# Routing of a group laid over two attention blocks, in an attention and mixture-of-experts kernel

## The chip, the cores and the metric

The kernel runs on one core of one Trainium2 chip. The metric is the device time of one execution in microseconds (us). The engines are PE (TensorE: matmuls), ACT (ScalarE), DVE (VectorE), POOL (GpSimd) and SP (SyncE, which issues most of the DMAs here).

## What is computed

```
qkv = x @ qkv_w + qkv_b                       # x: 2 x 2048 x 256, 16 heads of 16
q, k rotated; attn = softmax(q k^T / 4)       # 32 heads of 2048 x 2048
x1 = layernorm(x + (attn v) @ out_w + out_b)
n = layernorm(x1) * g1 + be1
x2 = x1 + n + (n @ mix_w + mix_b)
n2 = layernorm(x2) * g2 + be2
probs = softmax(n2 @ router_w)                # 8 experts, the best two are kept
out = sum over the two of p * (silu(n2 @ w1[e] + b1[e]) @ w2[e] + b2[e])
result = layernorm(x1 + x2 + out)             # "x1 +": residual around the whole second part
```

The 4096 tokens are sent to a table of rows sorted by expert; the experts then work on 71 tiles of 128 such rows.

## The kernel before, in words

**Phases.** `project` makes q, k and v, `maxima` is skipped for these inputs, and `attend_route_experts` does the rest: attention with the routing woven in, then the expert tiles, then the last norm. All of it is written out by hand: every engine has its own list of instructions, and semaphores join them.

**Attention.** The tokens are eight groups of 512. A block `i` is attention for group `i`: four units (quads of heads) of 32 steps, 128 steps `n` in all. At step `n` PE waits for exponential `n`, computes the scores of step `n + 3` (`score`, L1409, 8 matmuls into one of three PSUM buffers), and at every second step weighs one round of values (`weigh`, L1421, 4 matmuls that are recorded as 8, into the one output bank `at_po`). ACT does one exponential of 128x1024 a step (L1316). When a unit is weighed, DVE copies the output bank (`copy_out`, L1629) and later divides (`divide`: shuffle, reciprocal, product, L1637 to L1641). The first round of the next unit is weighed at its third step (g = 2) and needs that copy. SP then moves the unit into `heads_T` (`repack`, L995).

**Routing.** While block `i` runs, group `i - 1` is routed. On PE the routing is cut into pieces, each put after a step by a table: `OUT_AT` (eight pieces of the output product, two halves of four), `NORM_AT` (two transposes), `MIX_AT` (eight pieces), `SENT_AT` (two transposes of the second norm's rows), `ROUTER_AT` (two pieces of logits), `COUNT_AT` (counts). All share one PSUM bank, `small`; a job in it may start when DVE has read the one before (`small_read`). DVE's `route` adds each half to `total`, does three norms (`layer_norm`, L702 to L728), and chooses experts and places. POOL adds biases and residuals, copies values of the next unit (`copy_v`), and sends the rows by eight indirect DMAs (L1208). ACT does the router's exponential after step 104.

**After attention.** The last group's routing is set between expert tiles by `TAIL_AT`: a point `2i + 1` stands in tile `i` behind the first product of tile `i + 1` (`hide`, L1540), a point `2i + 2` behind tile `i`'s second product (`reduce`, L1553). A tile needs 1 MB of `w1`, in a ring of three, and 129 KB of rows. SP issues the weights of tile 2, then `b2`, then `repack` of the last unit, then the weights of tiles 3, 4 and 5 (L1078). 36 tiles are planned early, from the counts of groups 0 to 5 (`plan_early`).

Of the kernel before, what the change touches and what calls it, by code (L numbers as in the profile page):

```python
# [8 lines left out]
ALU = mybir.AluOpType  # L9
# [11 lines left out]
QC = S // 512  # L21
# [740 lines left out]
def attend_route_experts(nc, dram, keep):  # L762
# [14 lines left out]
    OUT_AT = {14: (0, 0), 16: (0, 1), 18: (0, 2), 20: (0, 3), 24: (1, 0), 28: (1, 1), 32: (1, 2), 33: (1, 3)}  # L777
    NORM_AT = {54: 0, 56: 1}
    MIX_AT = {60: (0, 0), 62: (0, 1), 64: (0, 2), 65: (0, 3), 68: (1, 0), 72: (1, 1), 76: (1, 2), 80: (1, 3)}
    SENT_AT = {92: 0, 94: 1}  # L780
    ROUTER_AT = {97: 0, 98: 4}
    COUNT_AT = 118
    LATE_V_FROM, LATE_V_EVERY = 8, 7
    with ExitStack() as stack:
# [128 lines left out]
        def piece(g):  # L913
# [19 lines left out]
        STEPS = 3 * LN_STEPS + 19  # L933
# [31 lines left out]
        def first_job(i):  # L965

            return LATE_JOBS + (i - 1) * JOBS
# [8 lines left out]
        with nc.Block() as block:  # L976

            @block.sync
            def _(sp):
# [5 lines left out]
                def repack(unit):  # L985
# [5 lines left out]
                    if i:  # L991
                        sp.wait_ge(small_done, first_job(i) + 2)
# [45 lines left out]
                for c in range(1, QC - 1):  # L1038
                    for q in range(UNITS):
                        load_q(0, c, q, c * UNITS + q)  # L1040
                        repack(c * UNITS + q - 2)
                    load_x(c)
                    keep_sum(c - 1)
                for q in range(UNITS):
# [3 lines left out]
                    repack((QC - 1) * UNITS + q - 2)  # L1048
                load_x(QC - 1)
                keep_sum(QC - 2)  # L1050
                load_second_k(1)
                sp.wait_ge(keep["stored_mid"][1], 16 * QC)
                for q in range(UNITS):
                    load_q(1, 0, q, QC * UNITS + q)
                    repack(QC * UNITS + q - 2)
                    if q < 2:
                        load_second_k(q + 2)
                load_x(QC)
                keep_sum(QC - 1)
# [23 lines left out]
                for c in range(1, QC - 1):  # L1083
                    for q in range(UNITS):
                        load_q(1, c, q, (c + QC) * UNITS + q)
                        repack((c + QC) * UNITS + q - 2)
                    load_x(c + QC)
                    keep_sum(c + QC - 1)

                for q in range(UNITS):  # L1090
                    load_q(1, QC - 1, q, LAST * UNITS + q)
                    repack(LAST * UNITS + q - 2)
                load_x(LAST)
# [5 lines left out]
                keep_sum(LAST - 1)  # L1099
# [13 lines left out]
                load_w1(2, 2)  # L1113
                sp.wait_ge(weighed, GROUPS * NR + LEAD)
# [56 lines left out]
            def _(pool):  # L1171
# [14 lines left out]
                def route(i, q):  # L1186

                    if q == 1:
                        pool.wait_ge(norm1_ready, i + 1)
# [776 lines left out]
```

## Time and profile before

| | us |
|---|---|
| three timed runs | 1661.41, 1660.91, 1659.82 (median 1660.91) |
| the profiled execution | 1657.93 |
| its span, first to last instruction | 1656.2 |
| attention, first exponential to the start of the last | 108.6 to 1089.6 |
| PE / ACT / DVE / POOL busy | 1601.3 / 1249.5 / 540.8 / 470.3 |

The profile records one execution. Its page gives busy time by engine, the chain of work that ended last, and the costliest groups of instructions; views of the trace give timelines, waits and sums over stretches. Matmul records overlap, since matmuls are pipelined, so how long a run of them holds PE is read from the starts of one run and the next, not from their lengths.

### The profile page before, as it was taken

The page shows a single profiled execution, that of the slowest core. Times are in us where ns is not written, and L with a number is a line of the kernel's source. Part 1 is how long each engine was busy: PE and PEld are TensorE (multiplying, and loading weights), DVE is VectorE, ACT ScalarE, POOL GpSimd, SP SyncE. Part 2 cuts the span into 40 slices and gives each one's busy share as a digit, 9 for nine tenths or more (in the row PEclk, how much of TensorE's full clock was granted, in tenths as well). Part 3 has the DMA queues.
Part 4 walks back from the last instruction along what each step waited for, and adds up shares of the span by engine and source line. Part 5 has one row for each costly group of instructions (what it writes and reads, how often), then busy time and mean ns, then how long its engine had stood idle before and what let it go on. Part 6 is the DMA issues. An engine that isn't in the chain of part 4 may idle for free.

```text
span 1656.2 us, 46008 instructions
## 1 busy us (share of the span) xinstructions
PE 1601.3 (97%) x18036; PEld 948.0 (57%) x18037; DVE 540.8 (33%) x1464; ACT 1249.5 (75%) x1879; POOL 470.3 (28%) x495
## 2 busy tenths in 40 slices
PE   7989999999999999999999999999999999999991
PEld 5544434434434434434433434468999999999990
DVE  5541215525525525515615535526110000000004
ACT  5669999999999999999999999953434444444442
POOL 4630011212212212212212212125455444444441
PEclk9999999999999999999999999999999999999996
DMA  5686110101102551300101101646577765666655
GB/s 175 204 174 88 47 41 11 54 28 28 53 28 67 92 92 39 105 29 28 53 28 31 50 28 34 242 162 179 161 198 203 201 188 166 187 181 173 186 136 209
DMA packets 108488, 181.20 MB, mean 109 GB/s; under 512 B 14121, under 2 KB 80361, under 8 KB 108137
## 3 DMA queue, kind: packets, MB, share of 16 engines
q1 hardware_dynamic: 94515, 160.47, 33.7%
q0 software_dynamic: 13296, 17.77, 5.5%
q8 instruction: 130, 2.13, 0.6%
q10 hardware_dynamic: 495, 0.41, 0.1%
q14 instruction: 52, 0.43, 0.1%
HBM read 134.07 MB, written 40.18 MB: 105 GB/s over the span
## 4 chain that ended last, share of the span: by engine, by line
PE 68%; issue 13%; DVE 5%; POOL 3%; ACT 2%; DMA 2%; POOLq 1%; DVEq 0%; ACTq 0%
PE at_s L1409 23%; PE at_po L1421 22%; PE at_s L1540 8%; PE at_s L1553 8%; PE at_small L1437 4%; ACT place L1316 2%; DMA rows_out<-place,at_v 1%; POOL place L1275 1%; PE at_small L1430 1%; POOL place L1270 1%; DVE cb_ln_stats L702 1%; DVE rt_ln_stats L702 1%; DVE rt_sent_rows L728 1%; PE at_po L1529 1%; DVE rt_sent_rows L1693 1%
## 5 line engine op out<-in xcount | busy, mean ns | idle before, releaser
L1316 ACT ACTIVATE place<-at_s 128x1024 f32<-128x1024 f32 x1024 | 956.4, 1112 | 25.9 <-PE at_s L1409 18.6
L1409 PE MATMUL at_s<-place 99*32 99x512 bf16 x8192 | 579.7, 380 | 6.5 <-PEq L614 3.8
L1421 PE MATMUL at_po<-place,at_v 128*32 128x512 f32 x4096 | 535.8, 593 | 0.0
L1409 PEld LDWEIGHTS at_s<-place 99*32 99x32 bf16 x8192 | 219.4, 96 | 442.1 <-issue 237.9
L1333 ACT ACTIVATE place<-at_s,b_turned 128x128 f32<-128x128 f32 x568 | 161.6, 368 | 141.5 <-PE at_s L1540 139.3
L1540 PEld LDWEIGHTS at_s<-ex_xT,place 128*128 128x128 f32 x2272 | 264.3, 192 | 5.8 <-issue 1.7
L1540 PE MATMUL at_s<-ex_xT,place 128*128 128x128 f32 x2272 | 265.7, 275 | 0.0
L1553 PE MATMUL at_s<-place 128*128 x1136 | 257.1, 379 | 1.0 <-issue 0.5
L1553 PEld LDWEIGHTS at_s<-place 128*128 128x128 f32 x1136 | 210.4, 190 | 27.4 <-issue 1.7
L1421 PEld LDWEIGHTS at_po<-place,at_v 128*32 128x32 f32 x4096 | 132.3, 110 | 96.1 <-issue 1.2
L1349 ACT ACTIVATE place<-at_s,at_v 128x256 f32<-128x256 f32 x71 | 33.6, 474 | 161.5 <-PE at_s L1553 158.4
L702 DVE BATCH_NORM_STATS2 cb_ln_stats<-place 128x6 f32<-128x256 f32 x32 | 10.7, 411 | 417.0 <-DMA place<-rows_out 417.0
L1175 POOL COPY at_v<-place 128x1024 f32<-128x1024 f32 x32 | 33.2, 1038 | 306.1 <-PE at_po L1421 258.8
L1280 POOL DMA_INDIRECT rows_out<-place,at_v x71 | 115.8, 1631 | 14.5 <-issue 13.2
L1208 POOL DMA_INDIRECT rows_in<-rt_sent_rows,rt_pos x64 | 62.3, 974 | 162.6 <-PE at_po L1421 157.1
L1639 DVE RECIPROCAL at_den<-at_den 128x512 f32<-128x512 f32 x32 | 107.3, 3353 | 1.1
L1270 POOL TENSOR_TENSOR place<-place,at_v 128x256 f32<-128x256 f32 x71 | 80.4, 1132 | 40.1 <-PE at_po L1529 36.6
L1653 DVE TENSOR_TENSOR late<-at_small,rt_total 128x512 f32<-128x512 f32 x32 | 22.1, 692 | 203.3 <-PE at_small L1437 203.3
L1275 POOL TENSOR_TENSOR place<-place 128x256 f32<-128x256 f32 x71 | 52.5, 739 | 81.6 <-ACT place L1349 78.7
L1629 DVE COPY at_o<-at_po 128x512 f32<-128x512 f32 x32 | 22.1, 692 | 159.9 <-PE at_po L1421 159.9
L1196 POOL TENSOR_TENSOR rt_total<-late 128x1024 f32<-128x1024 f32 x7 | 16.8, 2400 | 185.2 <-DVEq L1687 185.2
L1279 POOL TENSOR_TENSOR ex_spare_y<-rt_zero_rows 128x1 f32<-128x1 f32 x71 | 15.4, 217 | 173.3 <-DMA rows_out<-place,at_v 171.9
(222 smaller groups left out, 1022.8 us busy)
## 6 DMA issues: line engine op xcount, KB each, us to landing
place<-in_w SPq DMA_DIRECT2D x79, 1024.0 KB, 9.4
place<-k_parts SPq DMA_DIRECT2D x48, 256.0 KB, 4.6
place<-q_parts SPq DMA_DIRECT2D x186, 64.0 KB
at_v<-rows_in SPq DMA_DIRECT2D x71, 129.0 KB
place<-in_x SPq DMA_DIRECT2D x8, 512.0 KB, 4.7
at_heads_T<-at_o SPq DMA_DIRECT2D x128, 32.0 KB, 2.0
rt_x_in<-in_x SPq DMA_DIRECT2D x8, 512.0 KB, 4.1
rows_out<-rt_total SPq DMA_DIRECT2D x8, 512.0 KB, 3.9
```

The source lines that it names most:

```text
L1208: nc.gpsimd.indirect_dma_start(out=dram["rows_in"], in_=sent_rows[:, n, a, :], in_offset=None, out_offset=bass.IndirectOffsetOnAxis(ap=pos ...
L1270: nc.gpsimd.tensor_tensor(biased[:, :], b2[:, bass.ds(e, 1), :].rearrange("p o n -> p (o n)"), rows_now[:, r, D + 1:D + 2].broadcast_to([P ...
L1275: nc.gpsimd.tensor_tensor(y[:, u, :], y[:, u, :], biased[:, :], ALU.add).then_inc(y_ready, 1)
L1280: nc.gpsimd.indirect_dma_start(out=dram["rows_out"], in_=y[:, u, :], in_offset=None, out_offset=bass.IndirectOffsetOnAxis(ap=rows_now[:, r ...
L1316: nc.scalar.activation(probs[:, slot(i, n), :], scores(i, n)[:, :], ACT.Exp).then_inc(exp_done, 1)
L1333: last = nc.scalar.activation(hT[:, u, fc, :], p_h[u][:, fc, :], ACT.Silu, bias=keep["b1"][:, bass.ds(e, 1), fc])
L1409: last = nc.tensor.matmul(scores(i, n)[j:j + 32, s * 512:(s + 1) * 512], k_rows[0:ROWS_M, quad(q).start + h, kt * P + j:kt * P + j + 32], ...
L1421: last = nc.tensor.matmul(p_o[32 * h:32 * h + 32, :], v_one[q % 2][:, h, kt, :], probs[:, slot(i, q * NG + g), s * 512:(s + 1) * 512], sta ...
L1437: last = nc.tensor.matmul(out[j:j + 32, :], weights[:, j:j + 32], moving, start=start, stop=stop, skip_group_check=lone)
L1540: last = nc.tensor.matmul(p_h[u][:, fc, :], w1_now[slot][:, kc, fc * P:(fc + 1) * P], xT[:, u, kc, :], start=(kc == 0), stop=(kc == KC - 1))
L1553: last = nc.tensor.matmul(p_y[u][:, :], hT[:, u, fc, :], w2[:, bass.ds(e, 1), fc, :].rearrange("p o n -> p (o n)"), start=(fc == 0), stop= ...
L1639: v.reciprocal(den[:, :], den[:, :]).then_inc(den_ready, 1)
```

## The change

In block `i` two groups are now routed at once, each by a part. The front of group `i - 1` (output product, two norms, mixing, sums) stands at steps 24 to 56 and 80 to 116. The back of group `i - 2` (transposes of the second norm's rows, logits, counts) stands at steps 10 to 20 and at 40. Nearly all pieces are four steps apart. Block 1 has a front alone. After attention the back of group 6, then front and back of group 7 are set between expert tiles. The same operations are done, and each once for each group.

```diff
-    OUT_AT = {14: (0, 0), 16: (0, 1), 18: (0, 2), 20: (0, 3), 24: (1, 0), 28: (1, 1), 32: (1, 2), 33: (1, 3)}
-    NORM_AT = {54: 0, 56: 1}
-    MIX_AT = {60: (0, 0), 62: (0, 1), 64: (0, 2), 65: (0, 3), 68: (1, 0), 72: (1, 1), 76: (1, 2), 80: (1, 3)}
-    SENT_AT = {92: 0, 94: 1}
-    ROUTER_AT = {97: 0, 98: 4}
-    COUNT_AT = 118
+    SENT_AT = {10: 0, 14: 1}
+    ROUTER_AT = {18: 0, 20: 4}
+    ROUTER_EXP_AT = 27
+    COUNT_AT = 40
+    OUT_AT = {24: (0, 0), 28: (0, 1), 32: (0, 2), 36: (0, 3), 44: (1, 0), 48: (1, 1), 52: (1, 2), 56: (1, 3)}
+    NORM_AT = {80: 0, 84: 1}
+    MIX_AT = {88: (0, 0), 92: (0, 1), 96: (0, 2), 100: (0, 3), 104: (1, 0), 108: (1, 1), 112: (1, 2), 116: (1, 3)}
...
-        TAIL_AT = {3: (14, 16, 18, 20), 4: (24, 28, 32, 33), 9: (54,), 10: (56,), 11: (60, 62, 64, 65),
-                   12: (68, 72, 76, 80), 17: (92,), 18: (94,), 19: (97, 98), 26: (118,)}
-        SEND_ROUNDS = {0: (3, 5, 8, 10, 13, 15), 1: (18, 21)}
-        ROUTER_AFTER, SEND_AFTER = 10, 15
+        TAIL_AT = {3: ((LAST - 1, 10),), 4: ((LAST - 1, 14),), 5: ((LAST - 1, 18), (LAST - 1, 20)),
+                   7: tuple((LAST, at) for at in (24, 28, 32, 36)), 11: ((LAST - 1, COUNT_AT),),
...
+        FIRST_SENDS, LAST_SENDS = (25, 27, 29, 31), (34, 36, 42, 44)
+        ROUTER_AFTER = {3: LAST - 1, 15: LAST}
+        SEND_AFTER = {LAST - 1: 5, LAST: 18}
...
                 sp.wait_ge(scored, 2 * NG + LAST * NB + NB)
                 load_w1(2, 2)
+                keep_sum(LAST - 1)
                 sp.wait_ge(weighed, GROUPS * NR + LEAD)
                 sp.dma_start(b2[:, :, :], dram["b2"].partition_broadcast(P)).then_inc(loaded_b2, 16)
                 repack(GROUPS * UNITS - 1)
...
+                def route(i):
+
+                    beside = i < GROUPS
+                    front, back = i - 1, i - 2
+                    if back >= 0:
+                        choose(back)
+                    if beside:
+                        copy_out(i, 0)
...
+                    add_total(x1, 0)
+                    if back >= 0:
+                        give_places(back)
+                    if beside:
+                        divide(i, 0)
+                    if i == LAST:
+                        plan_early(nc, dve, making, carry, keep, scratch, planned)
+                    add_total(x1, 1)
...
+                    layer_norm(v, steps, x1, x1, w)
+                    if beside:
+                        copy_out(i, 1)
+                    layer_norm(v, steps, norm1, x1, w)
...
+                    if i == LAST:
+                        dve.wait_ge(x_turned, 2)
+                        v.tensor_copy(xT[:, :, :, :], p_x_first[:, :, :, :]).then_inc(xT_ready, 2)
+                        copy_out(i, 3)
+                    dve.wait_ge(sent, front + 1)
+                    layer_norm(v, steps, sent_rows[:, 0, :, 0:D], x2, w)
+                    if i < LAST:
+                        copy_out(i, 3)
+                    steps.then(v.tensor_tensor(norm1[:, :, :], sent_rows[:, 0, :, 0:D], spread("g2"), ALU.mult))
+                    v.tensor_tensor(sent_rows[:, 0, :, 0:D], norm1[:, :, :], spread("be2"), ALU.add
+                                    ).then_inc(norm2_ready, 1)
...
+                    if beside:
+                        divide(i, 3)
```

`repack` in a block now waits for six jobs of `small`, not two, since the output product ends at step 56 instead of 33. POOL's loop has the same operations in another order (`add_bias` and `double` at the start of a block, the sends between rounds 25 and 44).

How the instructions stand on three engines, names as in the program (`at_s` scores, `at_po` output bank, `at_small` the routing bank, `place` the large buffer of keys, probabilities and weights):

PE, the first two pieces of the output product in a block, before:

```order
L1437 MATMUL at_small<-rt_out_w,at_heads_T 32x256 x3
L1409 MATMUL at_s<-place 32x512 [waits at_exp_done]
L1409 MATMUL at_s<-place 32x512 x7
L1421 MATMUL at_po<-place,at_v 32x512 x4
L1409 MATMUL at_s<-place 32x512 [waits at_exp_done]
L1409 MATMUL at_s<-place 32x512 x7
L1437 MATMUL at_small<-rt_out_w,at_heads_T 32x256 x4
```

and now:

```order
L1467 MATMUL at_small<-rt_out_w,at_heads_T 32x256 x3
L1439 MATMUL at_s<-place 32x512 [waits at_exp_done]
L1439 MATMUL at_s<-place 32x512 x7
L1451 MATMUL at_po<-place,at_v 32x512 x4
L1439 MATMUL at_s<-place 32x512 [waits at_exp_done]
L1439 MATMUL at_s<-place 32x512 x7
L1439 MATMUL at_s<-place 32x512 [waits at_exp_done]
L1439 MATMUL at_s<-place 32x512 x7
L1451 MATMUL at_po<-place,at_v 32x512 x4
L1439 MATMUL at_s<-place 32x512 [waits at_exp_done]
L1439 MATMUL at_s<-place 32x512 x7
L1467 MATMUL at_small<-rt_out_w,at_heads_T 32x256 x4
```

The pieces were two steps apart and are four apart.

DVE, at the end of the last attention block, from the copy of the first expert rows on, before:

```order
L1794 COPY ex_xT<-at_small 128x512 [waits ex_x_turned]
L1629 COPY at_o<-at_po 128x512 [waits at_repacked1,at_weighed]
L1637 STREAM_SHUFFLE at_den<-at_o 128x512 [waits at_o_normed,at_o_copied]
L1639 RECIPROCAL at_den<-at_den 128x512 [waits at_den_ready]
L1641 TENSOR_TENSOR at_o<-at_o,at_den 128x512 [waits at_den_ready]
```

and now, first where the copy stands (18 short instructions of the norm lie between this place and the next):

```order
L1786 COPY ex_xT<-at_small 128x512 [waits at_small_read,ex_x_turned]
L1659 COPY at_o<-at_po 128x512 [waits at_repacked1,at_weighed]
L702 BN_STATS rt_ln_stats<-late 128x6 [waits rt_sent]
L702 BN_STATS rt_ln_stats<-late 128x6 x3
L715 TENSOR_TENSOR rt_ln_mean<-rt_ln_stats 128x4 [waits rt_step]
```

The second place, where the division stands:

```order
L728 TENSOR_SCALAR rt_sent_rows<-late,rt_ln_rstd,rt_ln_shift 128x256 x3
L1792 TENSOR_TENSOR late<-rt_sent_rows,rt_g 128x1024 [waits rt_step]
L1793 TENSOR_TENSOR rt_sent_rows<-late,rt_be 128x4x256 [waits rt_step]
L1667 STREAM_SHUFFLE at_den<-at_o 128x512 [waits at_o_normed,at_o_copied]
L1669 RECIPROCAL at_den<-at_den 128x512 [waits at_den_ready]
L1671 TENSOR_TENSOR at_o<-at_o,at_den 128x512 [waits at_den_ready]
```

The whole second norm of group 6 now stands between the copy and the division of the last unit.

SP, from the weights of tile 2 to those of tile 3, now:

```order
L1090 DMA place<-in_w 128x2x1024
L1016 DMA rows_out<-rt_total 128x4x256 [waits rt_kept]
L1130 DMA place<-in_b 128x2048 [waits at_weighed]
L1004 DMA at_heads_T<-at_o 16x512 [waits at_small_done,at_o_normed]
L1004 DMA at_heads_T<-at_o 16x512 x3
L1086 TENSOR_LOAD tile_expert
L1090 ISA [waits ex_hidden]
```

Before, the same stood there without the store of the kept sum (L1016): the weights of tile 3 are issued behind `repack`, which waits for the division (`at_o_normed`).

## Rows read from the trace of the kernel before

**Rows 1.** Windows, exponentials alone (L1316): block 1 and block 4: length, ACT busy (count)

```profile
227.96:350.89 122.93, 119.41 (x129) 1.00 0.10 28
...
597.88:720.99 123.11, 119.63 (x129) 1.00 0.25 66
```

**Rows 2.** The same view: block 4, steps 14 to 34 and steps 106 to 127

```profile
610.66:630.47 19.81, 19.20 (x21) 1.00 0.57 110
...
701.13:720.99 19.86, 19.86 (x23) 1.00 0.04 10
```

**Rows 3.** One line (L1316) in windows 701:703 and 718:721: min/median/max ns

```profile
L1316 ACT ACTIVATE place<-at_s x4: 1026/1040/1060, 700.2 to 702.9; 128x1024 f32<-128x1024 f32 x4
...
L1316 ACT ACTIVATE place<-at_s x4: 1273/1293/1312, 717.4 to 720.1; 128x1024 f32<-128x1024 f32 x4
```

**Rows 4.** Timeline of PE, quiet stretch: start, length, engine, line, tiles, count

```profile
702.79 1.07 PE L1409 MATMUL at_s<-place 99*32 99x512 bf16 x16
...
704.51 1.08 PE L1409 MATMUL at_s<-place 99*32 99x512 bf16 x16
```

**Rows 5.** Timeline of PE around one piece of the mix product

```profile
670.38 0.61 PE L1437 MATMUL at_small<-rt_mix_w,rt_turned 128*32 128x256 f32 x8
670.82 0.61 PE L1409 MATMUL at_s<-place 99*32 99x512 bf16 x8
```

**Rows 6.** Timeline of PE: transposes of the second norm's rows, one router piece

```profile
688.52 0.61 PE L1409 MATMUL at_s<-place 99*32 99x512 bf16 x8
689.29 0.66 PE L1430 MATMUL at_small<-identity,rt_sent_rows 128*128 128x128 f32 x4 [0.16 <-DVE rt_sent_rows L1693]
689.88 0.61 PE L1409 MATMUL at_s<-place 99*32 99x512 bf16 x8
...
695.16 0.43 PE L1437 MATMUL at_small<-rt_router_w,rt_turned 128*32 128x8 f32 x32
695.46 1.07 PE L1421 MATMUL at_po<-place,at_v 128*32 128x512 f32 x8
```

**Rows 7.** Timeline of DVE: one norm of 512 tokens, and the next one starting

```profile
509.57 1.41 DVE L702 BATCH_NORM_STATS2 rt_ln_stats<-late 128x6 f32<-128x256 f32 x4
511.01 0.17 DVE L715 TENSOR_TENSOR rt_ln_mean<-rt_ln_stats 128x4 f32<-128x4 f32 x1
...
515.82 1.08 DVE L702 BATCH_NORM_STATS2 rt_ln_stats<-late 128x6 f32<-128x256 f32 x3
```

**Rows 8.** Timeline of DVE: the norm's second step beside an addition on POOL

```profile
557.53 0.96 DVE L715 TENSOR_TENSOR rt_ln_mean<-rt_ln_stats 128x4 f32<-128x4 f32 x1
```

**Rows 9.** Timeline of DVE after the last attention block: shuffle, and last product, of the division

```profile
1096.33 0.73 DVE L1637 STREAM_SHUFFLE at_den<-at_o 128x512 f32<-128x512 f32 x1
...
1100.48 0.69 DVE L1641 TENSOR_TENSOR at_o<-at_o,at_den 128x512 f32<-128x512 f32 x1
```

**Rows 10.** Timeline of SP: the weights of tiles 3, 4 and 5

```profile
1104.36 4.48 SPq L1078 DMA_DIRECT2D place<-in_w  x3
```

**Rows 11.** DMA issues, window 1086:1130: count, KB each, median us to landing

```profile
place<-in_b SPq DMA_DIRECT2D x1, 1024.0 KB, 4.5
```

**Rows 12.** The page, part 6: the same columns, all weights of the experts

```profile
place<-in_w SPq DMA_DIRECT2D x79, 1024.0 KB, 9.4
```

**Rows 13.** Timeline of PE after attention: tile 1, from its first piece of routing

```profile
1108.22 1.93 PE L1437 MATMUL at_small<-rt_out_w,at_heads_T 128*32 128x256 f32 x32
1110.08 0.44 PE L1529 MATMUL at_po<-identity,at_v 128*128 128x128 f32 x2
...
1113.90 1.93 PE L1437 MATMUL at_small<-rt_out_w,at_heads_T 128*32 128x256 f32 x32
```

**Rows 14.** Windows: length, busy of PE, PEld, DVE, ACT, POOL, PEclk, DMA share, GB/s

```profile
104.00:106.00 2.00, 0.13 (x3) 0.00 (x0) 0.89 (x3) 0.00 (x0) 0.00 (x0) 1.00 0.46 115
...
108.50:112.00 3.50, 3.50 (x41) 1.30 (x33) 0.84 (x2) 3.45 (x5) 2.02 (x2) 0.51 1.06 152
...
1099.00:1101.00 2.00, 0.93 (x7) 0.49 (x6) 1.97 (x2) 1.11 (x4) 0.00 (x0) 1.00 0.13 53
```

More of the change, by code:

```diff
@@ L1058, in _ @@
                 load_x(QC)
-                keep_sum(QC - 1)
                 def load_w2(e):
@@ L1290, in _ @@
                         finish(i, r)
-                        for group, first in ((LAST - 1, 0), (LAST, SEND_AFTER)):
+                        if i == 0:
+                            double(LAST - 1)
+                        if i == 1:
+                            add_bias(LAST)
+                        for group, first in SEND_AFTER.items():
                             if first <= i < first + GT:
@@ L1317, in exponentials @@
                                              ).then_inc(exp_done, 1)
-                        if routed and n == 104:
-                            router(i - 1)
+                        if i >= 2 and n == ROUTER_EXP_AT:
+                            router(i - 2)
                 def router(i):
@@ L1361, in _ @@
                 nc.scalar.activation(spare_a[:, :], identity[:, 0:1], ACT.Exp)
-                exponentials(0, False)
-                for i in range(1, GROUPS):
-                    exponentials(i, True)
+                for i in range(GROUPS):
+                    exponentials(i)
                 act.sem_inc(y_scaled, 2)
@@ L1589, in route_last @@
                 def route_last(point):
-                    for at in TAIL_AT.get(point, ()):
-                        routed_job[0] += route(LAST, at, routed_job[0])
+                    for group, at in TAIL_AT.get(point, ()):
+                        routed_job[0] += route(group, at, routed_job[0])
                 pe.wait_ge(planned, 1)
@@ new lines, in turned_half, with add_total, choose @@
+                def turned_half(kc):
+                    job.arrived()
+                    v.tensor_copy(turned[:, kc, :], small[:, :]).then_inc(small_read, 1)
+                def add_total(out, half):
+                    job.arrived()
+                    tiles = slice(2 * half, 2 * half + 2)
+                    v.tensor_tensor(out[:, tiles, :], small[:, :].rearrange("p (a n) -> p a n", a=2),
+                                    total[:, tiles, :], ALU.add).then_inc(small_read, 1)
+                def choose(i):
@@ L1688, in route @@
-                    if not beside:
-                        v.tensor_tensor(total[:, :, :], x1[:, :, :], x2[:, :, :], ALU.add).then_inc(kept, 1)
-                    dve.wait_ge(sent, i + 1)
-                    layer_norm(v, steps, sent_rows[:, 0, :, 0:D], x2, w)
-                    steps.then(v.tensor_tensor(norm1[:, :, :], sent_rows[:, 0, :, 0:D], spread("g2"), ALU.mult))
-                    v.tensor_tensor(sent_rows[:, 0, :, 0:D], norm1[:, :, :], spread("be2"), ALU.add
-                                    ).then_inc(norm2_ready, 1)
@@ L1695, in route @@
-                    if not beside:
-                        v.tensor_tensor(sent_rows[:, 1, :, 0:D], norm1[:, :, :], spread("be2"), ALU.add
-                                        ).then_inc(doubled, 1)
-                    turned_half(0)
-                    turned_half(1)
-                    if beside:
-                        copy_out(i + 1, 2)
                     job.arrived()
```

200 lines of the change are left out of this document (99 added, 101 removed).

## The prediction

> **What bounds the kernel now.** I read the windows of the attention blocks first, since the change moves work inside them. Blocks 1 and 4 take 122.93 and 123.11 us for 128 exponentials, and ACT is inside one for about 119.5 of them [rows 1]. In block 4, 22 exponentials of a quiet stretch (no routing on PE but the counts) start in 19.86 us, 0.903 each, with ACT never idle; in the stretch from step 14 to 34, which holds the eight output pieces, 20 exponentials take 19.81 us instead of 18.06 [rows 2]. So ACT sets the pace where it is quiet and PE where there are pieces. ACT's true pace is a little slower than 0.903: along the quiet stretch the recorded length of one exponential grows from about 1.03 to 1.31 us [rows 3], 0.013 us each, so the ends lie 0.903 + 0.013 = 0.917 apart.
>
> Then PE's own need, from starts on its timeline. Two steps of scores and one round of values follow each other in 704.51 - 702.79 = 1.72 to 1.73 us, 0.865 a step [rows 4]. In a quiet stretch PE therefore has 0.917 - 0.865 = 0.05 us a step to spare. A piece of the output or mix product holds it for 670.82 - 670.38 = 0.44 us, the closest reading is 0.434 [rows 5]. A transpose piece holds it 689.88 - 689.29 = 0.59, a router piece 0.30 or a little less [rows 6]; the counts are eight small matmuls, 0.1. A block's PE work is 128 x 0.865 = 110.7, plus 16 x 0.434 = 6.9, 4 x 0.59 = 2.35, two router pieces 0.56 and the counts 0.1: 120.6 us. It lasts 123.1, so PE idles about 2.5 us a block. That, and no more, is what a better spacing can give back.
>
> **Where the 2.5 us are.** PE can bank spare time, because three score buffers let it run ahead of ACT, but only so much. In steps 14 to 34 the eight pieces cost 3.47 us, 20 steps spare 1.0, and the exponentials came 1.75 late [rows 2]: the bank held 3.47 - 1.0 - 1.75 = 0.7 us. A quiet stretch of L steps is worth 0.05 L up to 0.7, and the rest is idle. Before, steps 99 to 127 and 0 to 13 are quiet (43 steps, 2.15 - 0.7 = 1.45 idle), steps 34 to 53 (20 steps, 0.3), steps 81 to 91 (none). The transposes of the second norm's rows also wait for DVE: the scores start at 688.52 and need 0.43, the transposes start at 689.29, 0.3 us late, and a little again at the second [rows 6]: 0.4. Sum 2.15 of the 2.5; the other 0.3 I leave in both kernels.
>
> **The change, part by part.**
> 1. Blocks 2 to 7. Quiet are now steps 57 to 79 (23 steps, 0.45 idle) and 117 to 9 (21 steps, 0.35), and the norm's rows come ten steps early, so the 0.4 wait is gone. Idle falls by 2.15 - 0.8 = 1.35 us. Against it stands one new tight place. DVE's `copy_out` of unit 1 is now behind a norm that begins with the piece of step 56. A norm takes 515.82 - 509.57 = 6.25 us [rows 7]; with the addition before it and the copy behind it (0.7 each) and 0.3 of latency DVE is done 7.95 us after the piece. PE needs the bank at step 66, after ten steps of scores and four rounds, 10 x 0.434 + 4 x 0.862 = 7.8 us. I take 0.2 for it. Gain 1.15 us a block, 6.9 in six. Bounds: 0 and 2.5 a block.
> 2. Block 1 has a front alone. Its PE work is 120.6 - 1.8 = 118.8; its quiet steps add 1.95 of idle (0.45 as above; steps 0 to 23 and the end of the block 1.5): 120.8 instead of 122.93 [rows 1]. Gain 2.1.
> 3. The back of group 6 moves to the experts' part, where PE is the bound (of the span's 1656.2 us it is busy 1601.3): plus 2 x 0.59 + 0.56 + 0.1 = 1.8.
> 4. The start of the experts' part. SP issues the weights of tile 3 behind `repack`, which needs the last unit's division. That ended at 1100.48 + 0.69 = 1101.17 [rows 9], and the weights were issued at 1104.36 [rows 10], 3.2 later. Now the second norm of group 6 (6.25) and its two products with g2 and be2 (1.23 each) stand ahead of the division: it ends 8.8 later, at 1110.0, with 0.3 more if POOL's new addition `double` hinders it. The weights are issued at 1113.2 to 1113.5. A load of 1 MB just before took 4.5 us to land [rows 11]: 1117.7 to 1118.0. PE is there earlier. It reached tile 1's first point at 1108.22 [rows 13]; now a transpose piece stands there (0.59), then 1113.90 - 1110.08 = 3.82 of turning and second product, then 0.59 again: 1113.2. Before, the 3.7 us of output pieces and the early issue hid this load. PE now stands for 1118.0 - 1113.2 = 4.8 us. Bounds: 0, if the load finds its way earlier than I read, and 1113.5 + 9.4 - 1113.2 = 9.7 with the median landing of all these loads [rows 12]; I take the nearer row in time and size, 4.5.
> 5. The clock. PE was almost idle before attention (busy 0.13 of 2 us from 104 to 106), and right behind that pause it ran 3.5 us at a granted 0.51; a pause with 0.93 of 2 us busy at 1099 left it at 1.00 [rows 14]. A stand of 4.8 us is nearer to the first: half speed for some 3.4 us costs 1.7. Bounds 0 and 1.7.
>
> The Trainium skill bears on this last step ("TensorE: Matmul & The Clock Gate", section "Loop structure matters more than you think"): a loop in which the matmuls wait for a DMA lets the engine fall to the low clock. By that page the sum below holds the 1.7; by the pause at 1099 alone it would be -2.4 instead of -0.7. No run here yet shows a DMA wait of this length.
>
> Covered and priced at nothing: the sends (eight indirect DMAs) now run at rounds 25 to 44 and end before the last step in which they are needed; `copy_v` of unit 3, which came at about step 97 behind the norm's rows, comes at step 64; `repack` of units 0 and 1 waits for step 56 instead of 33, and behind it on SP stand loads of queries due at steps 93 and later; the router's exponential needs two more table loads on ACT between expert tiles, where ACT has room: of its 1249.5 busy us 8 x 119.5 are attention's, which leaves under 300 for the 566 us behind it. Were one of these covers gone, the first step behind it would wait for what is late, a copy of values of about 1 us at most.
>
> **Sum.** -6.9 - 2.1 + 1.8 + 4.8 + 1.7 = -0.7 us. The profiled execution took 1657.93, so its like would be 1657.2. It lies 3.0 below the median of the timed runs, 1660.91; I put the same difference on the median: **1660.2**. About 0.2% (3.3 us) is what a measurement can tell from no change. Without the clock loss the sum is -2.4, 1658.5, still inside.
>
> **Rivals.**
> - The stand does not happen (the load is issued or lands in time), the attention gain does: -6.9 - 2.1 + 1.8 = -7.2, 1653.7. For it: the blocks' part is safe arithmetic. Against: DVE's and SP's lists leave the weights no other way. Likewise with the stand but a full gain of 2.2 a block: -13.2 - 2.1 + 1.8 + 4.8 + 1.7 = -7.0.
> - The late weights cost more: with a landing of 9.4 us the stand is 9.7 and the sum -6.9 - 2.1 + 1.8 + 9.7 + 1.7 = +4.2, 1665.1. It decides from a landing of 8.5 us. Three loads now go out together, where before the third was issued 4.5 us after the first [rows 10]; but the first is first in the queue.
> - The output bank. DVE is late at step 66 in each block: if the norm there meets an addition on POOL, as one step did that took 0.96 us where it takes 0.17 elsewhere [rows 8, 7], 0.8 more is lost in each of seven blocks: -0.7 + 5.6 = +4.9, 1665.8. It decides from 0.57 a block. Against: POOL's additions are at steps 3 to 8, 76 to 82 and 118 in the new order.
>
> **How the numbers follow.** Forecast (gain and stand, with or without the clock) 0.44. Rivals of the first kind 0.28. Late weights at the longer landing 0.14, output bank 0.14. Faster by over 0.2% 0.29, within 0.43, slower 0.28. The range reaches from the first rivals to the last: 1653.5 to 1666.
>
> **What would show it.** Blocks 2 to 7 at 121.9 to 122.1 us and block 1 at 120.8; the exponentials late only in short bits after single pieces; no wait of the transposes for the norm's rows. DVE's copy of unit 1 starting within 0.3 us of PE's last round. In the experts' part a pause of PE of about 5 us ahead of tile 3's first product, its load issued behind `repack`, and a stretch at half clock behind it. The prediction is wrong if blocks stay at 123, if that load is issued before the division ends, or if another pause stands between tiles.

## The result, and the profile after

The changed kernel took 1665.91 us (median of six runs, 1664.13 to 1668.34) against 1660.60 for the kernel before (six runs, 1659.82 to 1661.76): ratio 1.0032, 95% interval 1.0021 to 1.0043. It is slower by 5.3 us. The forecast was 1660.2, no change. Timed again on another occasion the changed kernel took 1668.17 against 1659.84, ratio 1.0044 (1.0031 to 1.0057).

The profiled execution took 1664.94 us, span 1663.2, where the one before took 1657.93 and 1656.2: 7.0 more. That is above the 5.3 of the medians since the profiled execution before was a quick one (2.7 us under the median of the six timed runs, against 1.0 after). The exponentials divide this. The first starts at 108.64 us (before 108.60). The last starts at 1085.23 instead of 1089.58, so attention gained 4.3 us. From there to the end it takes 578.0 us instead of 566.7, so the experts' part lost 11.3.

**Attention.** Windows of blocks 1, 3, 4 and 5 of the changed kernel, exponentials alone (the columns of [rows 1]):

```profile
228.04:349.21 121.17, 119.08 (x129) 1.00 0.10 28
471.61:595.00 123.39, 119.86 (x129) 1.00 0.31 65
595.00:718.93 123.93, 119.95 (x129) 1.00 0.35 76
718.93:841.33 122.40, 119.86 (x129) 1.00 0.12 37
```

Block 1 has 121.17 for 122.93 [rows 1]. Blocks 2, 5 and 6 take 122.40. Blocks 3 and 4 take 1.0 and 1.5 more than that. Two things are to be found: why 122.4 and not the forecast 121.95, and what blocks 3 and 4 met. The waits of PE, of the changed kernel (engine, tile and line, who released it: us in total, times, longest), name the first:

```profile
PE at_s L1570 <- issue: 6.4, 1, 6.4
...
PE at_po L1451 <- DVE at_o L1659: 4.3, 7, 0.6
...
PE at_s L1583 <- ACT place L1364: 1.2, 2, 0.8
```

"Issue" means that the profile shows nothing that PE waited for. L1659 is `copy_out`. In seven blocks the values' first matmul waits for the copy of unit 1's bank, 0.6 us each as the profile counts it, and 1.1 from start to start. DVE in block 5 of the changed kernel shows how it comes:

```profile
781.15 2.11 DVE L728 TENSOR_SCALAR late<-late,rt_ln_rstd,rt_ln_shift 128x256 f32<-128x256 f32 x4
783.29 0.69 DVE L1659 COPY at_o<-at_po 128x512 f32<-128x512 f32 x1
```

The last of the four products (L728) by itself:

```profile
782.13 1.12 DVE L728 TENSOR_SCALAR late<-late,rt_ln_rstd,rt_ln_shift 128x256 f32<-128x256 f32 x1
```

POOL, then PE:

```profile
782.03 1.07 POOL L1190 COPY at_v<-place 128x1024 f32<-128x1024 f32 x1 [0.56 <-PE at_po L1451]
```

```profile
781.75 1.76 PE L1439 MATMUL at_s<-place 99*32 99x512 bf16 x24
784.13 1.07 PE L1451 MATMUL at_po<-place,at_v 128*32 128x512 f32 x8 [0.62 <-DVE at_o L1659]
```

24 score matmuls need three times 0.434, so the values could have begun at 781.75 + 1.30 = 783.05. They begin at 784.13, 1.08 late. The norm's four products took 2.11 us, and POOL's `copy_v` of unit 3 (782.03 to 783.10) began inside them. Only the last product is slow: it starts 0.1 behind POOL's copy, ends 0.15 behind its end, and takes 1.12 us, where each of the first three took 0.4. That the two overlap doesn't prove the cause; two experiments below test it.

The second thing is TensorE standing in the middle of one run of matmuls, in blocks 3 and 4, for nothing that the profile could name:

```profile
571.47 0.59 PE L1439 MATMUL at_s<-place 99*32 99x512 bf16 x5
572.69 0.83 PE L1439 MATMUL at_s<-place 99*32 99x512 bf16 x11 [0.62 <-issue]
...
609.06 1.03 PE L1451 MATMUL at_po<-place,at_v 128*32 128x512 f32 x7
611.04 0.59 PE L1451 MATMUL at_po<-place,at_v 128*32 128x512 f32 x1 [0.95 <-issue]
```

**The experts' part.** DVE, POOL (`double`), SP and PE of the changed kernel, from the second norm of group 6 on:

```profile
1098.19 1.23 DVE L1792 TENSOR_TENSOR late<-rt_sent_rows,rt_g 128x1024 f32<-128x1024 f32 x1
1099.45 1.52 DVE L1793 TENSOR_TENSOR rt_sent_rows<-late,rt_be 128x1024 f32<-128x1024 f32 x1
...
1100.89 0.73 DVE L1667 STREAM_SHUFFLE at_den<-at_o 128x512 f32<-128x512 f32 x1
1101.66 3.35 DVE L1669 RECIPROCAL at_den<-at_den 128x512 f32<-128x512 f32 x1
1105.05 1.88 DVE L1671 TENSOR_TENSOR at_o<-at_o,at_den 128x512 f32<-128x512 f32 x1
```

```profile
1103.41 2.96 POOL L1217 TENSOR_TENSOR rt_sent_rows<-late,rt_be 128x1024 f32<-128x1024 f32 x1
```

```profile
1106.96 2.42 SPq L1004 DMA_DIRECT2D at_heads_T<-at_o  x4
1110.13 2.66 SPq L1090 DMA_DIRECT2D place<-in_w  x3
```

```profile
1108.13 0.60 PE L1460 MATMUL at_small<-identity,rt_sent_rows 128*128 128x128 f32 x4
1115.14 5.08 PE L1570 MATMUL at_s<-ex_xT,place 128*128 128x128 f32 x27 [6.41 <-issue]
...
1120.71 0.72 PE L1467 MATMUL at_small<-rt_router_w,rt_turned 128*32 128x8 f32 x64
```

The last division ends at 1106.93, the weights of tile 3 are issued at 1110.13, and the first product that needs them starts at 1115.14, 5.0 us later. PE stands 6.4 us. Windows of PE (length, busy, granted clock, DMA share, GB/s) around it:

```profile
1108.00:1112.00 4.00, 0.73 (x6) 1.00 0.22 51
1112.00:1116.00 4.00, 0.86 (x4) 0.52 0.99 372
1116.00:1120.00 4.00, 4.00 (x25) 0.63 1.04 399
1120.00:1124.00 4.00, 3.57 (x81) 1.00 0.63 196
```

The clock falls to its low level (1.2 GHz) during the stand, and this lasts into the products of tile 3. In the kernel before these stood so:

```profile
1115.77 3.84 PE L1540 MATMUL at_s<-ex_xT,place 128*128 128x128 f32 x32
1119.44 0.38 PE L1529 MATMUL at_po<-identity,at_v 128*128 128x128 f32 x2
```

The 32 matmuls now took 1120.71 - 1115.14 = 5.57 us from their start to that of the next run, instead of 1119.44 - 1115.77 = 3.67: 1.9 lost.

### The profile page after: what moved, and what is told of

It is laid out like the page before. It is cut to its first block, busy times and chain, and to the rows that moved or that the text cites. A ratio compares the mean times of both kernels' runs of the same rounds, so it can differ in the third digit from the quotient of the medians.

```text
span 1663.2 us, 46004 instructions
## 1 busy us (share of the span) xinstructions
PE 1596.2 (96%) x18036; PEld 965.1 (58%) x18037; DVE 564.0 (34%) x1464; ACT 1253.2 (75%) x1881; POOL 477.9 (29%) x495
## 4 chain that ended last, share of the span: by engine, by line
PE 84%; issue 3%; DVE 2%; ACT 2%; DMA 1%; POOL 0%; POOLq 0%; ACTq 0%; DVEq 0%
PE at_po L1451 25%; PE at_s L1439 25%; PE at_s L1570 15%; PE at_s L1583 14%; PE at_small L1467 4%; ACT place L1347 2%; PE at_small L1460 1%; PE at_po L1559 1%; DMA rows_out<-place,at_v 1%; DVE cb_ln_stats L702 1%; DVE late L728 1%; DVE at_o L1659 0%; POOL place L1297 0%; DMA place<-rows_out 0%; DVE place L1847 0%
## 5 line engine op out<-in xcount | busy, mean ns | idle before, releaser
L1439 PEld LDWEIGHTS at_s<-place 99*32 99x32 bf16 x8192 | 232.9, 95 | 422.7 <-issue 271.7
L1364 ACT ACTIVATE place<-at_s,b_turned 128x128 f32<-128x128 f32 x568 | 161.9, 369 | 147.2 <-PE at_s L1570 146.9
L1583 PE MATMUL at_s<-place 128*128 x1136 | 257.2, 380 | 1.9 <-ACT place L1364 1.2
L1583 PEld LDWEIGHTS at_s<-place 128*128 128x128 f32 x1136 | 210.4, 190 | 28.4 <-issue 2.6
L1659 DVE COPY at_o<-at_po 128x512 f32<-128x512 f32 x32 | 22.1, 692 | 158.5 <-PE at_po L1451 145.5
L293 ACT ACTIVATE place<-p_qk,bias_qk 128x512 bf16<-128x512 f32 x32 | 21.8, 685 | 32.6 <-PE p_qk L504 25.1
```

The lines of the kernel that those rows point to most:

```text
L1364: last = nc.scalar.activation(hT[:, u, fc, :], p_h[u][:, fc, :], ACT.Silu, bias=keep["b1"][:, bass.ds(e, 1), fc])
L1439: last = nc.tensor.matmul(scores(i, n)[j:j + 32, s * 512:(s + 1) * 512], k_rows[0:ROWS_M, quad(q).start + h, kt * P + j:kt * P + j + 32], ...
L1583: last = nc.tensor.matmul(p_y[u][:, :], hT[:, u, fc, :], w2[:, bass.ds(e, 1), fc, :].rearrange("p o n -> p (o n)"), start=(fc == 0), stop= ...
```

## The experiments

My theory after the traces: (A) tile 3's weights are issued too late, and the stand costs itself, 6.4, and the clock behind it, 1.9; (B) the output bank at step 66 costs about half a us a block, since the norm in front of its copy runs beside `copy_v`; (C) the pieces moved to the experts' part cost the rest, 2 to 3 us. The rival to A was that the whole new order of DVE costs, not the weights; the rival to B that the blocks are bound elsewhere, and the wait is filled from spare time. All edits but those of the last two sections are to the changed kernel. Behind each measured time stands that of the kernel before, timed with it.

### Weights of tile 3 ahead of the last repacking

```diff
+                load_w1(W1_RING, 0)
                 repack(GROUPS * UNITS - 1)
-                for r in range(W1_RING, XR):
+                for r in range(W1_RING + 1, XR):
                     load_w1(r, r % W1_RING)
```

> Only edit to the changed kernel: SP issues the weights of tile 3 ahead of the last unit's repack instead of behind it. Theory A (queue order): the changed kernel stands 6.4 us on PE ahead of tile 3 and then loses 1.9 us in the product at half clock; both go, so about 8 us less than the changed kernel (1665.9 to about 1657.6), no PE pause over 1 us there and the clock at 1.00. Rival B (the load itself is slow because the DMA engines are full, or PE waits for the norm's rows there): the pause stays over 4 us and the time within 2 us of the changed kernel's. The attention blocks keep 122.4 us under both.

Measured: 1659.30 us (1656.01 to 1661.09) against 1660.34; ratio 0.9989 (0.9980 to 0.9998). SP and PE's windows of this kernel:

```profile
1095.71 0.38 SPq L1090 DMA_DIRECT2D place<-in_w  x1
1110.26 2.42 SPq L1004 DMA_DIRECT2D at_heads_T<-at_o  x4
1113.44 1.52 SPq L1090 DMA_DIRECT2D place<-in_w  x2
```

```profile
1108.00:1112.00 4.00, 4.00 (x24) 1.00 0.25 37
1112.00:1116.00 4.00, 4.00 (x89) 1.00 0.42 99
```

The stand is gone and the clock stays at 1.00, though the division and the repacking are as late as they were. From the last exponential to the end it takes 569.8 us instead of 578.0: 8.2 less, against 6.4 + 1.9 = 8.3. One line of SP's list moved carries the whole stand. What is left over the kernel before's 566.7 is 3.1 us, part C.

Two things blur these sums. Counted from the last exponential to the first product of tile 19, the changed kernel is 8.9 us later than this one, and this one 2.45 later than the kernel before; the other 0.7 stand behind the last tile, where this profile and two others (the division ahead of the norm, the late load) are about that much longer than the rest. And the time fell by 6.6 us (by ratio, 7 or 9, after the first or the second timing of the changed kernel), where I expected about 8. Block 0, which no edit touches, takes from 119.3 to 123.0 us from one profile to the next (119.4 in the changed kernel's, 123.0 in this one, 119.3 and 120.4 in two of one and the same kernel). So single profiles are compared here by stage, and not by their whole time.

### The division ahead of the norm

```diff
                         copy_out(i, 3)
+                        divide(i, 3)
                     dve.wait_ge(sent, front + 1)
...
-                    if beside:
+                    if i < LAST:
                         divide(i, 3)
```

> Only edit to the changed kernel: after the last attention block DVE divides the last unit before the second norm of group 6, as the kernel before did (it had no norm there). Theory A: the division ends about 9 us earlier, the weights of tile 3 are issued about 9 us earlier and the pause of 6.4 us goes; the second norm's rows come 4.9 us later (about 1105.9), so PE waits at tile 1's first transposes about 1.9 us. Sum about 6 us less than the changed kernel, about 1660. Rival B: the pause ahead of tile 3 stays over 4 us. Rival C (the wait for the norm's rows is hidden by other work): 8 us less, as with the load issued first.

Measured: 1663.80 us (1660.95 to 1665.25) against 1660.34; ratio 1.0018 (1.0009 to 1.0027). PE, SP and PE's windows:

```profile
1110.03 0.66 PE L1460 MATMUL at_small<-identity,rt_sent_rows 128*128 128x128 f32 x4 [2.08 <-DVE rt_sent_rows L1794]
1111.04 5.40 PE L1583 MATMUL at_s<-place 128*128 x16
```

```profile
1104.89 3.60 SPq L1090 DMA_DIRECT2D place<-in_w  x3
```

```profile
1110.00:1114.00 4.00, 3.83 (x14) 0.69 1.06 358
1114.00:1118.00 4.00, 4.00 (x25) 0.88 0.44 163
```

The weights are early, as in the kernel before, but now the second norm's rows are late, and tile 1's transposes wait 2.1 us for them. The clock falls behind this stand too: the 16 matmuls of L1583 last until 1116.28, 5.24 us where 1113.90 - 1110.36 = 3.54 were needed before. The tail is 574.2 us, 3.8 better than the changed kernel and 4.4 worse than with the weights moved. I had expected about 1660: the wait for the rows came as forecast (2.1 for 1.9), but not the 1.7 us of slow matmuls behind it, and the tail's gain of 3.8 shows only as 2.1 in the median. DVE has 14.2 us of work behind the last bank copy (the division 4.8, the norm with its two products 9.4), and whichever part goes second is waited for, unless what depends on it is taken out of the queue. The run shows one thing more: the division's last product stands alone here and takes 0.69 us (1099.97), as in the kernel before; in the changed kernel, beside POOL's `double`, it took 1.88.

### The bank copy inside the norm

```diff
     norm_scale(dve, steps, inp, w)
+    if between:
+        between()
...
-                    layer_norm(v, steps, x1, x1, w)
-                    if beside:
-                        copy_out(i, 1)
+                    layer_norm(v, steps, x1, x1, w, (lambda: copy_out(i, 1)) if beside else None)
```

> Only edit to the changed kernel: in each block DVE copies the output bank of unit 1 between the factors of the first norm and its four products, instead of behind them. Theory A (DVE's lateness at step 66 costs each block): PE's wait of about 1.07 us there goes and each of seven blocks becomes 0.3 to 0.8 us shorter (122.4 to about 121.9), 2 to 5 us in all. Rival B (the wait falls into a quiet stretch and is made good there, the missing gain is elsewhere): PE's wait goes too, but the blocks stay within 0.2 us of 122.4.

Measured: 1662.73 us (1660.60 to 1663.83) against 1660.34; ratio 1.0015 (1.0006 to 1.0024). DVE and PE in block 5 of this kernel:

```profile
779.42 0.69 DVE L1661 COPY at_o<-at_po 128x512 f32<-128x512 f32 x1 [0.96 <-PE at_po L1453]
780.03 1.52 DVE L730 TENSOR_SCALAR late<-late,rt_ln_rstd,rt_ln_shift 128x256 f32<-128x256 f32 x4
```

```profile
779.12 1.76 PE L1441 MATMUL at_s<-place 99*32 99x512 bf16 x24
780.70 1.03 PE L1453 MATMUL at_po<-place,at_v 128*32 128x512 f32 x8
```

The copy now waits for PE instead of the reverse. Blocks 2 to 6 take 121.84 us each, 0.56 less than 122.40, and block 1 takes 120.70. Neither block 3 nor block 4 had a stand in this profile. The experts' part is as slow as before (578.5 us).

### The values of unit 3 copied later

```diff
+                    if i >= 2:
+                        send_beside(i - 2, GT)
+                    else:
+                        pool.wait_ge(weighed, i * NR + 34 + LEAD)
                     copy_v(i * UNITS + 3, (i // QC, 3))
                     if i >= 2:
-                        for k in range(GT, GT + 2):
-                            send_beside(i - 2, k)
+                        send_beside(i - 2, GT + 1)
```

> Only edit to the changed kernel: POOL copies the values of unit 3 two to four steps later in a block, behind the next send, so that its copy no longer runs beside the four products that end the first norm on DVE. Theory A (the two engines slow each other): the four products take 1.38 us instead of 2.11, the bank copy comes 0.7 us earlier and PE's wait at step 66 falls from 1.07 to about 0.3; blocks 0.1 to 0.5 us shorter. Rival B (the products are slow for another reason): they still take 2.1 us and nothing moves.

Measured: 1662.86 us (1660.54 to 1664.64) against 1660.34; ratio 1.0018 (1.0009 to 1.0027). DVE and PE in block 5:

```profile
780.61 1.39 DVE L728 TENSOR_SCALAR late<-late,rt_ln_rstd,rt_ln_shift 128x256 f32<-128x256 f32 x4
782.04 0.69 DVE L1662 COPY at_o<-at_po 128x512 f32<-128x512 f32 x1
```

```profile
781.22 1.76 PE L1442 MATMUL at_s<-place 99*32 99x512 bf16 x24
782.87 1.07 PE L1454 MATMUL at_po<-place,at_v 128*32 128x512 f32 x8
```

Here the copy is still behind the whole norm, only without POOL beside it. The four products take 1.39 instead of 2.11. The values begin 782.87 - 781.22 - 1.30 = 0.35 late instead of 1.08, and blocks 2, 5 and 6 take the same 121.84 as with the other edit; block 3 met a delay of PE of 1.4 us at step 104, and block 4 took 122.2. So 0.35 us at this step are filled from spare time, and the 0.7 us that DVE lost beside POOL are what made the wait cost anything.

### The changed kernel again, and both edits together

> The changed kernel itself, unedited, timed again beside the two others. It read 1665.9 us against 1660.6 for the kernel before (ratio 1.0032). Theory (a stand ahead of the weights of tile 3, with half clock behind it, plus a wait for the output bank): 1663.5 to 1667, and its trace again shows TensorE standing 6 to 7 us before tile 3 and one wait of 1 us at step 67 of each block. The two short stands at step 104 of block 3 and step 15 of block 4 are, by the theory, chance meetings of TensorE with something in a full DMA stretch: they may be there or not, and the time moves by about 1 us each. Rival (the miss was chance between two lots of runs): within 0.1% of before.

Measured: 1668.17 us (1665.07 to 1670.81) against 1659.84; ratio 1.0044 (1.0031 to 1.0057). The same stand before tile 3 and blocks of 122.4 again; block 4 took 123.29, block 3 122.40. That is above my range of 1663.5 to 1667, and the miss isn't chance between two lots of runs. In this profile the tail took 580.6 us and not 578.0: PE is delayed several times, by up to 0.8 us, between tiles 29 and 43, for nothing that the profile names ("issue"). Block 0 took 1.6 more than in the first. What these delays in the tail are stays open.

> The changed kernel with both edits: SyncE issues the weights of tile 3 ahead of the last repacking, and the bank copy of unit 1 stands between the norm's factors and its products. Theory (the two costs are in different places and add): blocks 2 to 6 at 121.84 us and the tail behind the last exponential at 569 to 570.5 us; from the 1659.3 of the first edit alone, less the 3.1 that the second took off, 1656.2 us, range 1655 to 1657.5, ratio to before 0.9967 to 0.9982. Rival (the second edit moves the end of the last block ahead, so that weights, repacking and division of the tail come later against it, and part of the gain is waited away): a stand of 1 us or more ahead of tile 3 or of tile 1's transposes, and 1658 or more.

Measured: 1654.93 us (1653.59 to 1656.35) against 1659.84; ratio 0.9969 (0.9958 to 0.9980). Its tail is 569.3 us and its blocks 121.8 but for block 4 (123.2). The two costs lie in different places and add. Timed a second time:

> The changed kernel with both edits (weights of tile 3 ahead of the last repacking, bank copy of unit 1 inside the norm), as timed before at 1654.9 us (ratio 0.9969), run again beside the next one: 1653.5 to 1656.5. Its profile showed one stand of TensorE of 1.3 us at step 15 of block 4 and one of 1.1 at step 31 of block 0.

Measured: 1653.08 us (1650.70 to 1656.10) against 1660.18; ratio 0.9957 (0.9941 to 0.9973). With the two edits the change beats the kernel before by 5 to 7 us.

### The kernel before, with a late load

```diff
+                sp.wait_ge(y_done, 4)
                 for r in range(W1_RING, XR):
                     load_w1(r, r % W1_RING)
```

> The kernel before, with one wait added on SyncE: the weights of tile 3 are issued when TensorE has done the products of tile 1 (1113.98 us in its trace, against an issue at 1104.36). Nothing else is changed, so this prices a late load by itself. With a landing of 4.5 to 5.0 us TensorE stands from 1115.8 to about 1119.0: 3 to 3.6 us. Theory (a stand of that length costs itself and the half clock behind it, 1.9 us in the changed kernel behind 6.4 us): 1660.3 plus 4.5 to 5.6, so 1665 to 1666, with granted clock of 0.5 for some us behind the stand. Rival (only a stand of 6 us or more takes the clock down): 1663.3 to 1664, granted clock 1.00. Other rival (the late load isn't what the tail waits for): within 0.5 us of before.

Measured: 1666.08 us (1664.33 to 1668.37) against 1659.84; ratio 1.0034 (1.0022 to 1.0045). SP, PE and PE's windows:

```profile
1118.14 2.68 SPq L1078 DMA_DIRECT2D place<-in_w  x3
```

```profile
1117.34 1.94 PE L1438 MATMUL at_small<-rt_out_w,at_heads_T 128*32 128x256 f32 x32
1123.21 5.03 PE L1541 MATMUL at_s<-ex_xT,place 128*128 128x128 f32 x22 [3.94 <-issue]
```

```profile
1120.00:1124.00 4.00, 0.79 (x4) 0.70 1.00 389
1124.00:1128.00 4.00, 4.00 (x20) 0.50 1.05 355
```

Without anything of the change a load that lands 5.1 us after its issue, with a stand of 3.9 us, costs this kernel 6.2 us, between the 5.3 and the 8.3 that the whole change cost in its two timings. Against the kernel before, tile 3 starts 4.0 later and tile 4 a further 2.4: the clock's part. Landing and stand were each a little longer than I expected, and the cost 0.6 above the forecast 4.5 to 5.6.

### The second batch's keys loaded at once

From the kernel with both edits:

```diff
                 def load_second_k(q):
-                    for n in range(len(K_ORDER)):
-                        sp.wait_ge(scored, 2 * NG + (QC - 1) * NB + (q + 1) * NG + NG // 4 + n * (NG // 8))
-                        load_k(sp, dram, keep, 1, q, (n,))
+                    sp.wait_ge(scored, 2 * NG + (QC - 1) * NB + (q + 1) * NG + NG // 4)
+                    load_k(sp, dram, keep, 1, q)
...
-                    if q == UNITS - 2:
-                        load_second_k(0)
+                    if q >= UNITS - 2:
+                        load_second_k(q - (UNITS - 2))
                     repack((QC - 1) * UNITS + q - 2)
...
                 load_x(QC - 1)
-                load_second_k(1)
...
                     repack(QC * UNITS + q - 2)
+                    if q < 2:
+                        load_second_k(q + 2)
                     if q == 0:
                         keep_sum(QC - 2)
-                    if q < 2:
-                        load_second_k(q + 2)
```

> The same with the second batch's k loads changed on SyncE: their six pieces go out at once instead of every four steps, and those of units 1 and 2 go ahead of the repacking and of the sum that they stood behind, so that the DMA engines are not full when the next q rows are loaded. In the changed kernel TensorE stood 1 to 1.5 us at step 104 of block 3 and at step 15 of block 4, after 12 to 16 us with a DMA share of 1.0. Theory (those stands are TensorE's own instructions arriving late behind the loads): both go, blocks 3 and 4 at 121.84 us, 0.7 to 1.4 us less than the run beside it. Rival (they come at these steps whatever the loads do): blocks 3 and 4 still 0.7 to 1.4 us over 121.84, and the same time. Other rival (the moved loads delay the repacking and the sum): a new wait of a small product on a repacking, and a longer block 3.

Measured: 1655.13 us (1651.16 to 1660.62) against 1660.18; ratio 0.9971 (0.9960 to 0.9982), which overlaps that of the run beside it. Block 3 took 121.84, but it did so beside it too. Block 4 took 122.82: the delay at step 16 is gone and one of 0.84 us stands at step 31. So the delay moved with the loads and wasn't removed. No run shows what TensorE waits for there. The delays near step 104 of block 3 are in the profile of the kernel before as well (0.5 us), and others of 0.6 to 1.3 us stand at steps 32 and 60 of block 0 in several profiles.

The traces hold more on this than I used. Each lists its DMA packets, among them 130 of 16 KB on an instruction queue (q8). For the delay at step 16 of block 4, with times from the start of the block, where step 16 stands at 14.8:

| profile | such a packet ends at | delay of the next exponential |
|---|---|---|
| changed kernel | 14.61 | 1.42 |
| both edits, first and second | 14.60, 14.50 | 1.21, 1.07 |
| division ahead of the norm | 14.34 | 1.08 |
| weights of tile 3 first | 14.22 | 0.79 |
| changed kernel again | 14.09 | 0.77 |
| values later | 13.46 | none |
| bank copy inside the norm | 13.03 | none |
| k loads at once | 5.91 | none |

The later the packet, the longer the delay, but for a tie at 1.1. In the last profile a packet that ends at 24.8 to 26.3 in the others ends at 28.46, and the new delay stands just behind it, at 30. So the theory that TensorE's instructions arrive late fits all nine profiles, and what failed is the edit, which moved the late packet. No run changes the packets alone, so this is a strong match and not a proof. It is worth 1 to 2.5 us a run in blocks 3 and 4.

## Why the prediction was wrong

Against the profiled execution I forecast 1657.2, and it took 1664.9: 7.7 more. Attention gained 4.3 instead of 9.0 (4.7 short); the experts' part lost 11.3 instead of 8.3 (3.0 more). By the medians the miss is 6.0 us. Where the two costs lie, and the order of the queues, I had right; what failed are sizes. Two prices were too low: part 1's 0.2 us a block for the output bank, which cost 0.56, and part 4's stand of 4.8 us, which was 6.4. And the sum had no term for delays of PE inside blocks 3 and 4, which cost 2.5 us; they match late packets of an instruction queue, which is not proved. By its steps:

1. **Blocks 2 to 7, -6.9 forecast, -2.7 measured** (738.7 before, 736.0 after). The sum of idle time on PE was right (no run takes its parts one by one): without the wait at step 66 the six blocks take 730.1, a gain of 8.5, of which 0.6 is a delay in block 3 of the kernel before, so some 1.3 each; I had 1.35 before subtracting the bank. The failed line is the 0.2 for the output bank: it cost 0.56 a block, 3.4 in six. I had the mechanism as a rival, and argued it away since POOL's additions lie at other steps. It was to decide from 0.57 a block beyond the forecast's 0.2; it cost 0.36 beyond it, so alone it would not have turned the sum. POOL's `copy_v` lies there, at step 64. I named that step myself and priced it at nothing, looking only at when the values were needed and not at what DVE was doing beside it. The other 2.5 are the two delays in blocks 3 and 4, of which I forecast none. Of my signs, blocks of 121.9 to 122.1 us and a copy of unit 1 within 0.3 us of PE's last round did not show: the blocks took 122.4, and in block 5 the copy came 1.5 us behind the round.
2. **Block 1, -2.1 forecast, -1.8 measured**, and 120.70 without the bank's wait, where I had 120.8. Right.
3. **Group 6's back, +1.8 forecast.** By starts on PE the moved pieces hold it 1.6 us: a transpose piece takes 0.43 here, not 0.59. But with the stand and the clock loss taken away 2.3 to 3.1 us remain in the tail. Some 0.4 of that are longer waits of PE for ACT and issue than before; what is left, up to 0.4 between the tiles and in some profiles 0.7 behind the last one, no run explains. In the changed kernel itself another 0.4 follows the stand, as a longer wait for ACT (L1364, 0.8 us for 0.4).
4. **The stand, +4.8 forecast, 6.4 measured.** Place, order and cause as described, and moving that one load removed it. Three terms of it were off. Up to the division's shuffle DVE came 8.8 us later behind the bank's copy than before, just as forecast; then the division's product took 1.88 instead of 0.69 [rows 9], beside POOL's new `double`, 1.2 more where I had allowed 0.3. The load landed after 5.0 us, not 4.5 [rows 11]. And PE arrived 0.2 earlier than I counted. The 9.4 of [rows 12] had nothing to do with it: the same row of the changed kernel's page reads 5.5.
5. **The clock, +1.7 forecast, 1.9 measured.** The section "Loop structure matters more than you think" of the Trainium skill's page "TensorE: Matmul & The Clock Gate" warned of this, for a loop with such a wait in each turn. Here one wait was enough, and the traces agree: granted clock 0.52 from 1112 to 1116 us, while PE waited for the DMA, and 0.63 in the next 4 us. That the size came out so near is partly luck: the other stands cost 1.7 and 2.4. I also wrote that no run yet showed a DMA wait of this length. The trace of the kernel before has two of about this length, at the start of the program, and they point the other way. PE waits 4.8 and then 3.4 us for `x`, and the clock behind them is 1.00:

```profile
10.14 1.94 PE L479 MATMUL p_x<-identity,place 128*128 128x128 f32 x8 [3.44 <-DMA place<-in_x]
```

```profile
4.00:8.00 4.00, 1.94 (x8) 1.00 0.86 269
8.00:12.00 4.00, 1.86 (x9) 1.00 1.02 376
```

So two of the sum's terms were short, for one reason in the main: two engines lose beside each other, 0.7 us on DVE at step 64 of every block and 1.2 at the division. The delays of PE had no term at all; they are 2.5 of the 7.7, and the other lengthening of the tail 1.2. My range ended at 1666.0; the first timing is just inside it, the second outside. The chance of 0.28 that I gave to slower looks low in hindsight, since the bank, the division and the landing could each come out late far more easily than early; one outcome doesn't prove it.

What I would have had to see: [rows 8] shows a DVE step of 0.17 us take 0.96 beside POOL. I used it as a rival's price for additions only. Laid against every POOL operation in the new order, it would have given 0.7 to 0.8 at step 64 and at the division both, and a sum of about +5: 0.7 in each of seven blocks and 0.9 more at the division, on top of -0.7. That this is near the measured 5.3 would have been luck in part, for the bank cost 0.36 a block beyond my 0.2 and not 0.7, and the delays are not in it.

## To carry to other kernels

When work is moved, list for each place where one engine's copy or division is waited for what every engine that can slow it runs at the same step in the new order, large copies and not only additions, and price the race with the slow duration: in these traces the slowed instruction ended within 0.6 us of the end of POOL's. Where a load stands in a queue behind something it doesn't depend on, ask first whether it can go ahead of it: here that line was worth 6.6 us by the medians, more than the 4.3 us that attention gained by the new order. Price a stand of TensorE in a dense stretch with the clock behind it: here some 2 us on top, at stands of 2.1, 3.9 and 6.4 us.

## What the runs showed of the hardware

- A stand of 2.1 us (behind DVE), 3.9 us and 6.4 us (behind a load) each brought the granted clock down to its low level (1.2 GHz) for some us, and cost 1.7 to 2.4 us of slower matmuls. The length of the stand made no visible difference to the price. Not every pause did: in the kernel before, a stretch at 1099 with 0.93 of 2 us busy left it at 1.00 [rows 14], and so did a wait of 3.4 us at the start of the program.
- DVE loses time beside POOL: four products of 128x256 took 1.39 us alone and 2.11 beside a POOL copy of 128x1024; a 128x512 product took 0.69 alone and 1.88 beside a POOL addition of 128x1024. It looks like waiting rather than running slowly: one product of the four takes the whole loss and ends 0.15 us behind POOL's copy, and the step of 0.96 us of [rows 8] ends at 558.49, POOL's addition (556.08 to 558.46) 0.03 earlier.
- A load of 1 MB with two others right behind it landed after 5.0 and 5.1 us (issue to first product), in windows of 4 us with 372 and 389 GB/s. The load of the same size that took 4.5 [rows 11] had none of them right behind it; that this is the reason is not shown.
- TensorE can stand up to 1.4 us inside one run of matmuls, at the same step in several profiles of one kernel but not in all: at step 16 of block 4 and step 104 of block 3, where the loads of the second batch run, but also in block 0 and between expert tiles. At step 16 of block 4 there was none where a 16 KB packet of an instruction queue ended at 13.5 us of the block or before, and one of 0.8 to 1.4 us, growing with the lateness, where it ended at 14.1 to 14.6.
